# Expert slots of a two-layer AdaLN model on one core: additions' turn waits on separate cells, sixteen token places, first row loads read ahead

## What is computed

```python
h = layernorm(x) * (1 + ca) + sa
x = x + ga * linear_attention(h)        # layer 0: 32 heads of 64, relu on q and k, Wo, bias
h = layernorm(x) * (1 + cb) + sb
x = x + gb * moe(h)                     # layer 0: 8 experts of 256, each token goes to its best 2
h = layernorm(x) * (1 + ca) + sa
x = x + ga * (h + rmsnorm(y(h) @ W_out.T) * norm_w)   # layer 1: y is linear in h here
h = layernorm(x) * (1 + cb) + sb
x = x + gb * (sparsify_2of4(silu(h @ w_gate) * (h @ w_up)) @ w_down)   # layer 1
```

## Time and profile before

| what | value |
|---|---|
| median of 3 runs | 1878.19 us (1873.54 to 1880.81) |
| the profiled execution, its time and its span | 1875.54 us, 1873.8 us |
| TensorE busy, share of the span | 1787.5 us, 95% |
| DVE, ACT, POOL busy | 1173.4, 757.9, 723.7 us |
| granted TensorE clock, mean | 0.984 |
| first row load issued, first matmul of the slots, last addition issued | 988.37, 997.13, 1212.64 us |
| result read back from (start of the load) | 1217.57 us |
| gathers (L2601), additions (L2615), turn cells (L2612) on POOL | 39, 39, 111 |
| DMA moved | 216.35 MB, mean 115 GB/s |

### The profile page before, as it was taken

The page is one execution under the profiler, slowest core; times in us unless marked ns, Lnnn a source line. Parts: engine busy times, 40 slices in busy tenths (PEclk is TensorE's granted clock), DMA queues, the critical chain, the costliest instruction groups (busy, mean ns, idle before and its releaser), DMA issues.

```text
span 1873.8 us, 25682 instructions
## 1 busy us (share of the span) xinstructions
PE 1787.5 (95%) x8308; PEld 1401.4 (75%) x8308; DVE 1173.4 (63%) x2140; ACT 757.9 (40%) x1478; POOL 723.7 (39%) x698
## 2 busy tenths in 40 slices
PE   8889999999999999998898998979999999999998
PEld 5567878788878888876666776658778788787886
DVE  5557666676666766676754443557646657567476
ACT  2544555555454555534532222356632222213211
POOL 1433121211222211264344456635455536436342
PEclk9999999999999999999899999989999999999999
DMA  6101454535462544632368999730011001001001
GB/s 253 68 8 35 147 169 135 152 87 187 112 200 69 174 140 146 186 105 92 113 226 253 282 286 282 163 118 18 28 35 51 12 29 51 29 10 56 7 29 73
DMA packets 99955, 216.35 MB, mean 115 GB/s; under 512 B 8504, under 2 KB 33096, under 8 KB 98336
## 3 DMA queue, kind: packets, MB, share of 16 engines
q1 hardware_dynamic: 77744, 166.60, 28.1%
q0 software_dynamic: 11520, 28.96, 6.4%
q10 hardware_dynamic: 10608, 19.74, 3.2%
HBM read 123.93 MB, written 91.35 MB: 115 GB/s over the span
## 4 chain that ended last, share of the span: by engine, by line
PE 73%; DVE 9%; DMA 6%; issue 5%; POOL 3%; ACT 3%; POOLq 0%; ACTq 0%; DVEq 0%; SPq 0%
PE bank L810 21%; PE bank L812 20%; PE bank L811 20%; DMA u_d<-yt,sm 5%; PE bank L1051 3%; PE bank L1217 2%; PE bank L997 2%; PE bank L914 1%; DVE hh L2345 1%; DVE rr L2009 1%; PE bank L1058 1%; POOL gbt L2601 1%; PE bank L999 1%; POOL mark L2612 1%; PE bank L884 1%
## 5 line engine op out<-in xcount | busy, mean ns | idle before, releaser
L2009 DVE RECIPROCAL rr<-rr 128x256 f32<-128x256 f32 x128 | 218.8, 1730 | 0.0
L2444 POOL TENSOR_TENSOR x<-x,tmp 128x512 f32<-128x512 f32 x76 | 116.2, 1533 | 258.8 <-DVE tmp L2002 258.8
L810 PE MATMUL bank<-W1a,hT 128*128 128x512 f32 x512 | 209.4, 409 | 3.4 <-DVE hT L1931 3.4
L810 PE MATMUL bank<-hT,W1b 128*128 128x512 f32 x512 | 208.8, 408 | 2.4 <-DVE hh L2302 2.4
L811 PE MATMUL bank<-hT,W1b 128*128 128x512 f32 x512 | 204.0, 398 | 0.0
L812 PE MATMUL bank<-hT,W1b 128*128 128x512 f32 x512 | 203.8, 398 | 0.0
L812 PE MATMUL bank<-W1a,hT 128*128 128x512 f32 x512 | 201.1, 393 | 0.0
L811 PE MATMUL bank<-W1a,hT 128*128 128x512 f32 x512 | 200.3, 391 | 0.0
L2302 DVE TENSOR_TENSOR hh<-hh,bank 128x512 f32<-128x512 f32 x64 | 43.8, 688 | 183.4 <-PE bank L812 146.7
L2369 POOL TENSOR_TENSOR W<-stage,W 128x1024 fp32r<-128x1024 f32 x32 | 77.2, 2412 | 184.4 <-ACT W L1300 182.1
L2034 DVE SCALAR_TENSOR_TENSOR kt<-bank,kt 128x256 fp32r<-128x256 f32 x128 | 50.5, 395 | 152.8 <-ACT vt L1439 152.6
(11 more groups left out here) (299 smaller groups left out, 4555.3 us busy)
## 6 DMA issues: line engine op xcount, KB each, us to landing
hs_d<-bor SPq DMA_DIRECT2D x24, 1548.0 KB, 12.0
ws_d<-W SPq DMA_DIRECT2D x48, 512.0 KB, 6.1
WB<-ws_d SPq DMA_DIRECT2D x8, 3072.0 KB
stage<-wa SPq DMA_DIRECT2D x32, 512.0 KB, 5.5
stage<-wbe SPq DMA_DIRECT2D x24, 512.0 KB, 4.2
stage<-wdn SPq DMA_DIRECT2D x24, 512.0 KB, 3.9
hg<-hs_d ACTq DMA_DIRECT2D x39, 258.0 KB
mw<-wmod SPq DMA_DIRECT2D x5, 1024.0 KB, 5.0
```

The source lines that it names most:

```text
L810: pe.matmul(o, lhs(HI), rhs(HI), start=start, stop=False, **kw)
L2009: dve.reciprocal(rr[:, pair, h], rr[:, pair, h]).then_inc(r_rec, 1)
L2444: pool.tensor_tensor(xt, xt, tmp[:, (key + t) % 2, :], ALU.add).then_inc(ring_done, 1)
```

## The change

Four things change: the three cells of `turned` take the turn additions, whose own ends are waited for at the next slot and no longer at once; `sm` has 16 places; ACT reads the six values of the first three row loads as soon as `tab_rows` is set, before it waits for the scattered sequences; and the tiny activations between the first loads are no longer waited for.

```diff
-NS = 8
+NS = 16
...
+        turned = sb("turned", [1, NY - 1])
...
                 def rows_load(i):
-                    if i >= 3:
+                    if i >= EARLY:
                         act.wait_ge(th_full, i - 2)
                         act.wait_ge(sm_done, i - 2)
-                    at_ = act.value_load(tab[0:1, TAB_ROW, i:i + 1], min_val=0, max_val=HS_ROWS - MT)
+                    at_ = early_at[i] if i < EARLY else first_row(i)
                     act.dma_start(hg[:, i % 3, :], hs_d[bass.ds(at_, MT), :]).then_inc(hg_full[i % 3], 16)
 
+                def first_row(i):
+                    return act.value_load(tab[0:1, TAB_ROW, i:i + 1], min_val=0, max_val=HS_ROWS - MT)
+
                 act.wait_ge(tab_rows, 1)
+                early_at = [first_row(i) for i in range(EARLY)]
+                batches = [act.value_load(tab[0:1, TAB_LAST, i:i + 1], min_val=1, max_val=2) for i in range(EARLY)]
                 for b in range(NB - 1):
                     act.wait_ge(sc_done[b], 16 * 2 * NT)
                 act.activation(passed_on[0:1, EARLY:EARLY + 1], tiny[0:1, 0:1], ACT.Copy).then_inc(rows_there, 1)
                 for i in range(EARLY):
-                    batches = act.value_load(tab[0:1, TAB_LAST, i:i + 1], min_val=1, max_val=2)
-                    act.wait_ge(rows_there, batches)
-                    act.activation(passed_on[0:1, i:i + 1], tiny[0:1, 0:1], ACT.Copy).then_inc(rows_asked, 1)
-                    act.wait_ge(rows_asked, i + 1)
+                    act.wait_ge(rows_there, batches[i])
+                    act.activation(passed_on[0:1, i:i + 1], tiny[0:1, 0:1], ACT.Copy)
                     rows_load(i)
...
                     if i > NY:
                         first = pool.value_load(tab[0:1, TAB_FIRST, i:i + 1], min_val=0, max_val=16)
-                    for j in range(max(0, i - NY + 1), i):
+                    if turns[0] > 0:
+                        pool.wait_ge(turn, turns[0])
+                    for k, j in enumerate(range(max(0, i - NY + 1), i)):
                         pool.wait_ge(us_done[j % NY], added(j) if j < NY else first + (added(j) - 16))
                         turns[0] += 1
-                        pool.tensor_tensor(mark[:, 3:4], mark[:, 1:2], mark[:, 2:3], ALU.add).then_inc(turn, 1)
-                        pool.wait_ge(turn, turns[0])
+                        pool.tensor_tensor(turned[:, k:k + 1], mark[:, 1:2], mark[:, 2:3], ALU.add).then_inc(turn, 1)
                     pool.wait_ge(y_evac, i + 1)
```

More of the change, by code:

```diff
@@ L514, in build @@
         rows_there = sem("b_three_or_four_batches_scattered")
-        rows_asked = sem("b_first_slot_rows_there")
         w_all = sem("b_expert_loaded")
```

## The result

The changed kernel takes 1867.11 us, the median of 13 runs (1862.74 to 1876.80), beside 1877.26 us for the kernel before in as many runs. The ratio of the two is 0.995, with a 95% interval of 0.9938 to 0.9962: 9.4 us less, between 7 and 12.

The account below looks back on a forecast made before the run. POOL's chain of cells and additions was taken to end the slots; +2.2 (first row loads) - 2.7 (last six intervals) - 6.0 (half the rest) = -6.5 us, from 1878.19 to 1871.7 us, range 1862 to 1880.

Parts of the forecast that it names:

- One sign: In the changed profile, DVE no longer waits for additions in `tokens` but waits longer in `weighted`.
- What bounds the kernel: In the slots, POOL and its additions set the stage's end; a microsecond off this chain is one off the end.
- The cells, 0.45 us per short interval: POOL between additions without waiting for the last to land: 0.22 before the addition, 0.23 in three cells; 27 such intervals.
- The last six intervals, 2.7 us: POOL's additions from 1190 to 1217, no expert loaded any more: 6 x 0.45 us had in full.
- One half of the rest, 6.0 us: Of the other 11.9 us saved on POOL, half reaches the end, since expert loads fill the DMA engines.
- Sixteen places, in the half: DVE's stall moves behind `product`, freeing TensorE: between nothing and 8.7 us, counted within the 6.0 us.
- The first row loads, +2.2 us: ACT's start of the slots: six value loads at 0.7 us delay the first row load 2.2 us, all reaching POOL's first addition.
- The unawaited activations: Between ACT's first row loads: three ends of a 0.20 us activation saved, all behind the first load, worth nothing.
- The whole gain: Rival: all POOL's saving arrives as TensorE brings expert loads forward; +2.2 - 14.6 = -12.4, 1865.8 us; chance 0.25.
- The DMA engines do not end every long interval: Rival claimed they do, so only the last six intervals gain: +2.2 - 2.7 = -0.5, 1877.7 us; chance 0.20.
- The cells did not keep their distance: Rival claimed they do on POOL, only the last wait being saved: +2.2 - 4.9 = -2.7, 1875.5 us; chance 0.07.
- The slower rival: ACT's six value loads at 0.98 us delay the first row load 3.9 us: +2.6, 1880.8 us; chance 0.06.

Follow-up runs that it names:

- e1: Only the cells' own awaited ends removed from the kernel before (8 places, value loads as before): 1865.23 us beside 1874.83.
- after: The profiled kernel with the whole change, against the kernel before: median 1867.11 us beside 1877.26, profiled execution 1864.96 us.
- e12: The changed kernel with the end of the last cell in each slot awaited again before the addition: 1869.43 us, beside 1866.72 for the changed kernel.
- e6: The kernel before with the weight loads of experts 3 to 7 cut from 3 MB to 256 KB (stale weights): 1862.26 us beside 1874.15.
- e7: The changed kernel with the weight loads of experts 3 to 7 cut from 3 MB to 256 KB (stale weights): 1857.36 us.
- e2: Only sixteen places in place of 8 in the kernel before: 1874.83 us, the same median as the kernel before.
- e8: The changed kernel with 8 places again, cells and read-ahead kept: 1867.21 us against 1867.17 for the changed kernel.
- e9: The changed kernel timed once more as yardstick: 1867.17 us, ratio 0.9953 to the kernel before.
- e5: The changed kernel with only the first row load's two values read ahead, the other four between the loads: 1866.19 us, ratio 0.9952 to the kernel before.
- e11: The changed kernel timed again as yardstick: 1866.72 us, ratio 0.9954 to the kernel before.
- e10: The changed kernel without the read-ahead (cells and sixteen places), run once more: 1864.99 us, ratio 0.9952 to the kernel before.
- e3: Only the six value loads read ahead and the unawaited activations, in the kernel before: 1877.53 us beside 1874.83.

## Why the prediction was right, and where its terms were off

The time lies in the range (1862 to 1880) and at the edge of the forecast's own (1867 to 1876), 4.6 us under the predicted one; a time below 1868.8 had been given 0.32. The forecast's mechanism is the one that happened: short intervals shrink, and long ones give part of it back. That the sum came so near is in part luck: the work saved was sized too small, and the share of it that is kept too large. One sign was missed as well: DVE's wait in `weighted` did not grow (23.3 us in both).

**What bounds the kernel.** Right for the part that gained. POOL's chain of cells and additions set the end: the cells alone (e1) give the whole gain, and a microsecond at the read-back is one at the end, in all profiles.

**The cells, 0.45 us per short interval.** The mechanism was right and the size too small. The three cells came as worked out (0.48 forecast, 0.47 to 0.48 measured). The failed term is the gap before the addition, taken as 0.31 from the gap between an indirect DMA and the next. That was the wrong neighbour: behind a cell which nobody waits for the gap is 0.16, and the 0.30 is the gap behind an indirect DMA. So a short interval of this kind saves 0.59 us, and the 27 save 109.4 - 90.9 = 18.5 us, 0.68 each, for the 12.2 of the sum. The mean is above 0.59 because the short intervals of before were not all alike: some had 0.1 us more between their cells, and the last three, without gathers, save 0.8 each. All in all POOL's chain lost 18.5 + 11 x 0.37 = 22.6 us of its own time, not 14.6.

**The last six intervals, 2.7 us.** From the first addition of them to the last, 1191.53 to 1212.64 before and 1184.65 to 1201.21 after: 21.1 and 16.6 us, so 4.5 us, by the same mis-sized term. POOL's timeline of after there, where gathers have ended, shows the shortest interval of all, 1.96 us:

```profile
1199.25 1.56 POOL L2619 DMA_INDIRECT u_d<-yt,sm  x1 [0.23 <-POOL turned L2617]
1200.28 0.70 POOL L2617 TENSOR_TENSOR turned<-mark 1x1 f32<-1x1 f32 x3
1201.21 1.56 POOL L2619 DMA_INDIRECT u_d<-yt,sm  x1 [0.23 <-issue]
```

**One half of the rest, 6.0 us.** A single profile has to be read with care here: the eight profiles of kernels with the new cells and whole expert loads, after among them (e12 left out), lie between 187.4 and 193.3 us from the first to the last addition, with a mean of 189.5; the three with the old cells lie at 199.4 to 200.6, mean 200.2. So 10.7 us are kept. Less the 4.5 of the last six, 6.2 us remain, as the 6.0 of the sum. But they remain of 22.6 - 4.5 = 18.1 us, not of 11.9: a third was kept and not a half, and two errors met. The long intervals took the rest back: their sum is 90.9 us on average with the old cells and 98.7 with the new ones, though each has 0.37 us less of POOL's work in it.

**Why they give it back.** The forecast said the DMA engines. e6 shows it for the kernel before: small expert loads shorten only the long intervals, by 14 us. But e7 shows a second bound right behind, TensorE, which the forecast had named only as the 13.1 us that it could get back. In after TensorE is idle for 6.3 us of the 203.

The place of the gain says more. A load of an expert's weights starts when TensorE has done with the expert three before, and the start of the last of them hardly moved. Before and after, the last load and the window up to it:

```profile
L667 SPq DMA_DIRECT2D WB<-ws_d x1: 368/368/368, 1125.3 to 1125.3; - x1
997.00:1126.00 129.00, 123.43 (x600) 97.81 (x599) 59.12 (x151) 35.78 (x77) 65.17 (x98) 1.00 0.90 268
L667 SPq DMA_DIRECT2D WB<-ws_d x1: 368/368/368, 1126.1 to 1126.1; - x1
997.00:1126.00 129.00, 125.02 (x596) 99.48 (x595) 59.19 (x155) 36.41 (x78) 65.97 (x102) 0.98 0.92 270
```

Of the 13.1 idle us of TensorE before, only 5.6 lie ahead of this load, so there was little by which the loads could come forward. From the table's entry to the last load it is 140.4 us on average in the three profiles with the old cells and 139.0 in the eight with the new ones; from there to the last addition it is 85.1 and 76.9. Counted by slots: from the first addition to the 20th, shortly before the last load, 3.2 us are kept of the 10.4 that POOL has less to do, and from the 20th to the last 7.5 of 12.2. So less than a third is kept while experts are loaded, and most of the gain is had behind that, the 4.5 us of the last six intervals included. This is read from the profiles; no experiment moved TensorE's work in that stretch.

**Sixteen places, in the half.** Between 0 and 8.7 us were allowed, and it is 0 within some 2 us (e2, e8). The forecast's reason, that TensorE could do the next gate and up products meanwhile, is true and worth nothing: the wait comes back one step later, at `at_lo`, and the stage is not TensorE's to end.

**The first row loads, +2.2 us.** At its own place the term was right: 2.3 us later, with 0.75 us per value load for the 0.7 taken. The Trainium skill (DMA: Bandwidth & Descriptors, Latency and other measured facts) gives a `tensor_load` about 600 ns at least, and the prediction set this aside. Alone it does not hold: ACT's 39 loads of `tab` have a median of 0.289 us in after. But the time of all six, 4.49 us, is what the estimate from the Trainium skill had given (4.5): the six loads come with their register operations and the gaps between them. That "all of the 2.2 us goes to POOL's first addition" fits the mean of the profiles, 25.2 us behind the table's entry without the read-ahead and 27.3 with it, though the two groups overlap (see the end). What no run shows is that all of it goes on from there to the end. The three pairs with and without read-ahead that were timed beside the same runs differ by 1.0 us (e9, e5), by 1.7 (e11, e10) and by 2.7 (e3 and the kernel before), each time towards slower, and each time the intervals overlap or hold zero. So the read-ahead costs something between nothing and 3 us, and more than that the runs don't tell.

**The unawaited activations.** Taken as nothing; they were not tried apart from the read-ahead, and what the two cost together is said above.

**The rivals.** The whole gain did not arrive (22.6 us less work, 10.7 kept), though its price, 1865.8, lies nearer to the measured time than the forecast. That is an accident: with the gap as measured it would have been +2.3 - 22.6, some 1858. The DMA engines do not end every long interval, or after would be at +2.3 - 4.5, some 1876. By the Trainium skill (DMA: Bandwidth & Descriptors, SWDGE vs HWDGE vs iDMA) a DMA engine takes turns between its queues. The additions did get on beside the expert load, but no row of any run tells the turns apart. The cells did not keep their distance. The slower rival's place was right, its price per value load (0.98) was not.

## What to carry to other kernels

Take the price of a gap from a row with the same two neighbours: the kind of instruction before it decides, and whether somebody waits for that instruction's end. Where an engine falls back at some points and catches up between them, ask what ends the points; what is saved between them is kept only as far as those ends move, here for about a third. Ask too where in the stage the idle time of the other engine lies: a sum over the stage hides that it had next to none to give where the ends were fixed. A buffer that takes away a wait of one engine is worth nothing while the wait comes back at the next hand-over and another engine sets the end.

## What the runs showed of the hardware

Starting an indirect DMA on POOL takes 0.16 us behind a cell nobody waits for (0.23 in the last intervals, where no gathers run), 0.28 behind three cells whose last end is waited for, 0.53 behind a single awaited cell, and 0.30 behind another indirect DMA.

The start of the slots scatters, and the clock of TensorE with it. Where TensorE had sat idle for 4.2 to 4.9 us before the first transposes (before, after, e1, e6, e9), they took 1.09 us instead of 0.63 and the granted clock over 994 to 1000 us was 0.50 to 0.76 of full; where it had been idle for 2.5 us or less (e2 to e5, e8, e10, e11) it was 1.00. In e7 and e12, idle for 3.0 us, it was 0.72. 0.50 is the lower level, 1.2 GHz. The window from 994 to 1000 us of after:

```profile
994.00:1000.00 6.00, 5.47 (x11) 3.25 (x12) 3.07 (x9) 2.66 (x5) 1.83 (x3) 0.50 0.14 48
```

The same window of e5:

```profile
994.00:1000.00 6.00, 5.85 (x24) 3.48 (x23) 3.36 (x9) 3.04 (x6) 1.57 (x3) 1.00 0.48 156
```

TensorE is busy alike, with 11 matmuls in the one and 24 in the other. The idle time did not follow the read-ahead (e3, e8 and e11 read ahead and had 1.5, 0.6 and no idle time), but what other work TensorE still had when the rows came. So the first addition comes 23.7 to 26.6 us behind the table's entry without the read-ahead and 25.3 to 30.1 with it (e6, e7 and e12 aside), and both the late load and the low clock are in these. No experiment held the clock and moved the load, so how the two share the scatter stays open. The clock scatters later too: over 1054 to 1074 us it was 0.83 in e2 and e3, 0.91 in e8 and e9, and 1.00 in all the others, which is one more reason to go by several profiles.
